# A gated cross-attention block on one core: scores transposed, probabilities kept in whole fp32, values weighed one step later

## Chip, cores and metric

One core of a Trainium2 chip runs the whole kernel. The metric is the device time of one launch in microseconds (us), the median of the runs shown. The launch holds every stage: query projection, attention, output projection and a small feed-forward part.

## What is computed

`x` is (8, 56, 512), the context is (8, 1500, 512), all in fp32. The attention has 32 query heads in 8 groups of 4; a group shares one key head and one value head of width 128. The mask here is all zeros, but it is added as given.

```python
q = rope(layernorm(x) @ wq)            # 8 x 56 rows, 32 heads of 128
k = rope(context @ wk)                 # 8 x 1500 rows, 8 heads of 128
v = context @ wv                       # 8 x 1500 rows, 8 heads of 128
attn = softmax(q k^T / sqrt(128) + mask)
x = x + tanh(g_xattn) * (attn v) @ wo
x = x + tanh(g_ffn) * lora_moe(layernorm(x))   # 4 experts, rank 16, top 2
```

## The kernel before, in words

**Precision.** A product that needs more than one reduced-precision pass is made of three: every operand is split into a high half (a copy rounded to fp32r) and a low half (the difference), and `PASSES` (line 45) sums hi x hi, low x hi and hi x low. K, V and the scores are made so. The high half is written by ScalarE and the low half by VectorE or GpSimd, mostly straight from PSUM.

**Stages.** `query_part` projects the queries of all batches and stores them by head group in DRAM. `attention_part` then runs 64 steps, one for each of 8 batches `b` and 8 groups `g`. `output_part` projects the stored attention output with `wo`, group by group, and adds the feed-forward part.

**One attention step** (`step`, one copy of it in each engine's program) works on group g and prepares the next one:
- *K parts* (`k_part`, L805): keys of the next group, 3 chunks of 500 positions (written K00 to K23: chunk, then quarter of the contraction), 3 matmuls of 500 columns each, 36 in all. ScalarE copies the halves of a chunk crosswise (swap, L715), VectorE multiplies by cosine and sine and adds (cos L938, sin L942, rot L948), ScalarE writes the high half (K, L720), GpSimd the low half (`k_low`, L673).
- *V parts* (`v_part`, L821): values for a pair of groups, made over two steps, on average 72 matmuls of 256 columns a step. ScalarE writes the high half (L734), VectorE the low half (`v_low`, L962).
- *Scores* (`scores`, L845): 112 rows (2 heads x 56 queries) by 500 keys, 6 such pieces (S0 to S5) of 3 matmuls. VectorE adds the mask and takes the row maximum in the same operation (L1002), then the maximum of three chunk maxima (L1007). ScalarE takes exp over 1500 columns with the row sum as a by-product (L760).
- *Transposes* (`transposes`, L857): the probabilities lie with queries on the partitions, and the product with the values needs keys there. Six groups T0 to T5 of four fp32 transposes each bring them to PSUM. ScalarE writes the high half (L785), VectorE the low half (L1027).
- *Weighing the values* (`weigh`, L874): for each of 12 tiles of 125 keys one matmul of v_hi against both halves (448 columns) and one of v_lo against the high half (224 columns); PV0 to PV5 are two tiles each. ScalarE and VectorE add the two 224-column results (L770, L1033).
- *Normalising* (`normalise`, L987): the row sums are inverted with the queries on the partitions (L1012), written to DRAM and read back spread over 128 partitions (`inv_dram`, two DMAs a step on SP's queue), and multiply the result of the step before. It is stored to DRAM for the output stage.
- In the last step of a batch (kind "turn") the context of the next batch is transposed as well, C0 to C11 of four transposes each (`c_transposes` L832, split at L724 and L953).

**What sets the order.** Each engine works through its own list for the kind of step: `PE_STEP`, `ACT_STEP`, `DVE_STEP` (from line 66 on), with kinds "even", "odd", "turn", "pre", "last" and a "first" list ahead of all. The lists are written out; a word is one piece of work, and every engine takes its list strictly in order, waiting on semaphores. PSUM is shared as rings of two banks: `k_banks`, `sv_banks` (scores and values), `t_banks` (context and probability transposes), `o_banks`. A ring's bank is handed back by `k_free`, `sv_free`, `t_free`, `o_free`.

**SP's queue** in a step: store the attention result of the step before (`store_attn`, L613), write and reread the inverted sums (L642), load the queries of the step after next, load two context tiles of the next batch. In the last batch it also starts the loads of the output stage.

**The output stage** (`project_group`, L1082): per group 4 heads x 4 column blocks x 3 matmuls of 448 columns; groups 0 and 1 are done within the last attention step (words O0 and O1 there), groups 2 to 7 after it. `split_low` on VectorE and `wo_high`/`attn_high` on ScalarE split each group's operands (L1059, L1053, L1071, L1065).

## Time and profile before

| | |
|---|---|
| runs shown | 2008.92, 2008.79, 2007.59 us; median 2008.79 us |
| profiled execution, first to last instruction (span) | 2005.4 us; its own launch time isn't listed, the medians lie 3.4 us above the span |
| TensorE matmul / weight load busy | 1976.7 us (99%) / 1775.9 us (89%) |
| VectorE / ScalarE / GpSimd busy | 1235.0 us (62%) / 1034.3 us (52%) / 311.6 us (16%) |
| mean granted TensorE clock | 0.996 |
| attention steps: first score matmul to first score matmul of the last step | 124.0 to 1882.2 us, 63 steps |
| HBM traffic | 76.6 MB read, 15.8 MB written |

How to read it: the records of matmuls overlap, because TensorE is pipelined. The duration of one record therefore says little, and the distance from one start to the next says what a matmul costs in a stream. In the tables of operands the moving operand stands first, then the stationary one; `112*125 112x112` is a stationary operand of 112 partitions by 125 columns and a moving one of 112 columns. A matmul of two plain fp32 operands (not fp32r) appears as two records, and a transpose of fp32 data as one: lines 1290 and 1275 issue 4 and 16 matmuls and have 8 and 32 records, line 857 issues 1536 transposes and has 1536. "PEclk" or "granted clock" is 1.00 at 2.4 GHz and 0.50 at 1.2 GHz.

### The profile page before, as it was taken

What the parts mean: (1) busy time and instruction counts of PE and PEld (TensorE: products, weight loads), DVE (VectorE), ACT (ScalarE), POOL (GpSimd) and SP (SyncE); (2) the same over time, 40 slices, a digit from 0 to 9 for tenths busy, and PEclk for the clock granted to TensorE, in tenths of its full rate; (3) what the DMA queues carried; (4) which work ended last, traced back from release to release, by engine and by line L of the source; (5) the groups of instructions that cost most, each with busy time, mean ns of one, the idle gap of its engine ahead of it and who ended that gap; (6) DMA issues with size and microseconds to landing.
All of it is one profiled execution on the core that took longest, in us unless ns stands there. A gap on an engine that the chain in (4) does not pass through costs nothing. (4 is left out here: it accounts for less than half of the span.)

```text
span 2005.4 us, 32965 instructions
## 1 busy us (share of the span) xinstructions
PE 1976.7 (99%) x12404; PEld 1775.9 (89%) x12404; DVE 1235.0 (62%) x2639; ACT 1034.3 (52%) x1754; POOL 311.6 (16%) x227
## 2 busy tenths in 40 slices
PE   7999999999999999999999999999999999999998
PEld 7989889988899988998899988998899998999786
DVE  6766556666666666666666666666665666566544
ACT  6655555554545555555644555455554555455532
POOL 5511111111111111111111111111111111111200
PEclk9999999999999999999999999999999999999998
DMA  7611212111211212221111112221111112121270
GB/s 227 248 56 35 35 18 44 35 31 20 43 10 33 36 17 44 35 35 20 39 19 25 35 20 41 36 35 20 39 25 26 28 20 41 36 33 15 48 263 19
DMA packets 74904, 94.41 MB, mean 47 GB/s; under 512 B 22692, under 2 KB 49444, under 8 KB 74760
## 3 DMA queue, kind: packets, MB, share of 16 engines
q1 hardware_dynamic: 73752, 86.01, 20.4%
q10 hardware_dynamic: 1008, 6.42, 0.8%
q8 instruction: 97, 1.59, 0.4%
q14 instruction: 47, 0.39, 0.1%
HBM read 76.64 MB, written 15.77 MB: 46 GB/s over the span
## 5 line engine op out<-in xcount | busy, mean ns | idle before, releaser
L673 POOL TENSOR_TENSOR k_lo<-k_work,k_hi 128x500 fp32r<-128x500 f32 x192 | 244.1, 1285 | 1541.0 <-ACT k_hi L720 1513.3
L821 PE MATMUL low_banks<-wv_hi,cT_hi 128*125 128x256 f32 x1536 | 443.1, 288 | 0.0
L821 PE MATMUL low_banks<-wv_hi,cT_lo 128*125 128x256 f32 x1536 | 431.0, 281 | 0.0
L821 PE MATMUL low_banks<-wv_lo,cT_hi 128*125 128x256 f32 x1536 | 430.9, 281 | 0.0
L1027 DVE TENSOR_TENSOR pT<-t_banks,pT 125x448 fp32r<-125x448 f32 x384 | 236.0, 622 | 242.8 <-ACT pT L785 242.8
L1002 DVE CUSTOM_DVE_ANT_0 prob<-low_banks,mask_t 112x500 f32<-112x500 f32 x384 | 259.1, 678 | 178.2 <-PE low_banks L845 176.9
L785 ACT ACTIVATE pT<-t_banks 125x448 fp32r<-125x448 f32 x384 | 205.1, 543 | 309.2 <-PE t_banks L857 308.2
L760 ACT ACTIVATE prob<-prob,neg_max 112x1500 f32<-112x1500 f32 x128 | 198.6, 1552 | 289.7 <-DVE neg_max L1007 288.9
L805 PE MATMUL low_banks<-cT_hi,wk_hi 128*128 128x500 f32 x768 | 312.0, 406 | 0.0
L805 PE MATMUL low_banks<-cT_hi,wk_lo 128*128 128x500 f32 x768 | 298.6, 389 | 0.0
L805 PE MATMUL low_banks<-cT_lo,wk_hi 128*128 128x500 f32 x768 | 298.3, 388 | 0.0
L821 PEld LDWEIGHTS low_banks<-wv_hi,cT_hi 128*125 128x125 f32 x1536 | 285.1, 186 | 4.3
L821 PEld LDWEIGHTS low_banks<-wv_hi,cT_lo 128*125 128x125 f32 x1536 | 285.8, 186 | 2.7
L821 PEld LDWEIGHTS low_banks<-wv_lo,cT_hi 128*125 128x125 f32 x1536 | 285.2, 186 | 0.0
L874 PE MATMUL o_banks<-pT,v_hi 125*128 125x448 f32 x768 | 272.4, 387 | 1.8 <-DVE pT L1027 0.7
L715 ACT ACTIVATE k_work<-low_banks 64x500 f32<-64x500 f32 x384 | 223.6, 582 | 14.4 <-PE low_banks L805 5.8
L857 PE MATMUL t_banks<-ident,prob 112*125 112x112 f32 x1536 | 220.6, 270 | 0.9 <-DVE pT L1027 0.9
L857 PEld LDWEIGHTS t_banks<-ident,prob 112*125 112x125 f32 x1536 | 207.0, 188 | 14.3 <-DVE pT L1027 1.0
L962 DVE TENSOR_TENSOR v_lo<-low_banks,v_hi 125x512 fp32r<-125x512 f32 x192 | 132.2, 689 | 137.0 <-ACT v_hi L734 137.0
L734 ACT ACTIVATE v_hi<-low_banks 125x512 fp32r<-125x512 f32 x192 | 114.3, 595 | 192.5 <-PE low_banks L821 192.3
L874 PE MATMUL o_banks<-pT,v_lo 125*128 125x224 f32 x768 | 193.5, 265 | 0.0
L805 PEld LDWEIGHTS low_banks<-cT_lo,wk_hi 128*128 128x128 f32 x768 | 144.5, 188 | 29.9
(136 smaller groups left out, 2910.2 us busy)
## 6 DMA issues: line engine op xcount, KB each, us to landing
stage<-in_ctx_dram SPq DMA_DIRECT2D x72, 250.0 KB
attn_by_head<-attn SPq DMA_DIRECT2D x65, 112.0 KB, 1.7
wq_raw<-in_L_xattn_wq_dram SPq DMA_DIRECT2D x7, 1024.0 KB, 7.2
q_raw<-q_by_head SPq DMA_DIRECT2D x64, 112.0 KB, 4.9
inv_b<-inv_by_head SPq DMA_DIRECT2D x64, 112.0 KB, 5.1
head_rows<-in_ctx_dram SPq DMA_DIRECT2D x24, 250.0 KB
mask_t<-in_mask_BxSxS_ff_dram SPq DMA_DIRECT2D x16, 328.1 KB
stage<-in_L_xattn_wo_dram SPq DMA_DIRECT2D x4, 1024.0 KB, 7.3
```

The costliest lines, as they stand in the source:

```text
L673: nc.gpsimd.tensor_tensor(k[1][:, c * SC:(c + 1) * SC], k_rot[:, s], f32(k[0][:, c * SC:(c + 1) * SC]), ALU.subtract).then_inc(k_lo, 1)
L715: nc.scalar.activation(k_swap[lo * HALF:(lo + 1) * HALF, s], k_banks[(1 - lo) * HALF:(2 - lo) * HALF, s, 0:SC], ACT.Copy).then_inc(k_swapp ...
L734: nc.scalar.activation(v[0][:, 2 * m:2 * m + 2, :], sv_banks[0:ST, m % 2, :].rearrange("p (t n) -> p t n", t=2), ACT.Copy).then_inc(v_hi, 1)
L760: nc.scalar.activation(prob[n][:, :], prob[n][:, :], ACT.Exp, bias=neg_max[:, n:n + 1], accum_out=row_sum[:, n:n + 1]).then_inc(p_ready, 1)
L785: nc.scalar.activation(pT[:, n % PT_SLOTS, :, 0, :], t_banks[0:ST, t_bank, 0:2 * GQ].rearrange("p (t n) -> p t n", t=2), ACT.Copy).then_in ...
L805: mm = nc.tensor.matmul(k_banks[:, s, 0:SC], w[0][a][:, d, g * DH:(g + 1) * DH], cT[m][:, d, c * SC:(c + 1) * SC], start=(d == 0 and n == ...
L821: mm = nc.tensor.matmul(sv_banks[0:ST, m % 2, t * PAIR:(t + 1) * PAIR], cT[a][:, d, tile * ST:(tile + 1) * ST], w[1][mv][:, d, g * DH:g * ...
L857: mm = nc.tensor.transpose(t_banks[0:ST, s, col:col + ROWS], prob[h][:, (2 * j + t) * ST:(2 * j + t + 1) * ST], ident[0:ROWS, 0:ROWS])
L874: mm = nc.tensor.matmul(o_banks[:, g % 2, 0:(2 - a) * GQ], v[a][:, 2 * j + t, (g % 2) * DH:(g % 2 + 1) * DH], probs, start=(first and a == ...
L962: nc.vector.tensor_tensor(v[1][:, 2 * m:2 * m + 2, :], sv_banks[0:ST, m % 2, :].rearrange("p (t n) -> p t n", t=2), f32(v[0][:, 2 * m:2 * ...
L1002: nc.vector.tensor_tensor_reduce(prob[h][:, c * SC:(c + 1) * SC], sv_banks[0:ROWS, n % 2, 0:SC], mask_t[:, c * SC:(c + 1) * SC], 1.0, LOWE ...
L1027: nc.vector.tensor_tensor(pT[:, n % PT_SLOTS, :, 1, :], t_banks[0:ST, t_bank, 0:2 * GQ].rearrange("p (t n) -> p t n", t=2), f32(pT[:, n % ...
```

## The change

The scores are made with the keys on the partitions: the stationary operand is a tile of 125 keys, the moving one the 224 query columns (4 heads x 56). Each of the six score pieces is now two key tiles, 6 matmuls of 224 columns, and the ring is `t_banks` instead of `sv_banks`. VectorE adds a mask that has been transposed once per batch (two items "B" of three transposes each in "first" and "turn", copied by VectorE), and writes the sums into one fp32 array `weights` (125 partitions x 25 slots x 224 columns, used by two steps in turn). The transposes of the probabilities and both splits of them are gone.

The maximum over the keys is found in four operations: over the first 8 tiles (max0), over the other 4 with the partial result (max1), transposed by TensorE to have queries on the partitions (MT, two transposes), reduced there ("rows", 2 x 125), and spread back over the partitions by two transposes of a broadcast column (MB). VectorE subtracts it from the scores in three operations of 896 columns (sub0 to sub2), ScalarE takes exp in three operations of 896 columns (exp0 to exp2). VectorE adds the 12 tiles in one `tensor_reduce` (total), and a matmul with ones (SUM) adds over the partitions and spreads the sums in one go; VectorE inverts them (inv) on 224 columns and multiplies (norm). The trip of the inverted sums through DRAM is gone.

Values and probabilities enter the last product in whole fp32: 12 matmuls of 224 columns into one bank, no low half of V, no second output half to add. This product, its sums, "inv" and "norm" of step n stand in the lists of step n+1 (words with a leading z). V parts V30 and V31 move from "first" to "zero", the kinds "zero" (g = 0), "pre" and "pre_last" (g = 6) get lists of their own. In the last step the product of that step follows within the same list, the heads of the output stage's first two groups are spread out (O00 to O13), and SP's loads for output group 3 stand behind the last store of the attention result. GpSimd's program changes only in the order of the last two steps. The mask is loaded as rows of 125 numbers.

```diff
 PE_STEP = {
...
-    "odd": ("S0 S1 K00 K01 S2 S3 K02 K03 S4 S5 K10 K11 K12 K13 K20 K21 T0 K22 T1 K23 T2 PV0 V00 T3 V01 PV1 PV2 V10 "
-            "T4 V11 PV3 V20 V21 T5 V30 V31 PV4 PV5"),
...
+    "zero": ("zPV0 K00 S0 S1 S2 zPV1 zPV2 zPV3 S3 S4 K01 S5 K02 K03 zPV4 zPV5 V30 K10 MT K11 K12 MB K13 zSUM V31 "
+             "V40 K20 K21 V41 K22 K23 V50 V51"),
+    "odd": ("K00 S0 S1 zPV0 zPV1 S2 S3 zPV2 S4 zPV3 zPV4 zPV5 K01 S5 zSUM K02 K03 K10 MT K11 K12 K13 MB V00 V01 "
+             "K20 K21 K22 K23 V10 V11 V20 V21"),
+    "even": ("zPV0 S0 zPV1 S1 S2 zPV2 S3 S4 K00 zPV3 zPV4 zPV5 zSUM S5 K01 K02 K03 K10 MT K11 K12 MB K13 V30 V31 "
+             "V40 K20 K21 K22 K23 V41 V50 V51"),
...
+    "turn": ("S0 S1 zPV0 S2 S3 zPV1 C0 S4 C1 zPV2 zPV3 S5 zPV4 C2 C3 zPV5 zSUM B0 K00 B1 C4 K01 K02 K03 MT C5 C6 "
+             "V00 MB C7 C8 V01 C9 K10 K11 K12 C10 V10 C11 V11 K13 K20 K21 K22 K23 V20 V21"),
...
+    "last": ("S0 S1 zPV0 S2 zPV1 S3 zPV2 S4 zPV3 S5 zPV4 zPV5 zSUM O00 MT O01 MB O02 O03 PV0 PV1 PV2 PV3 PV4 PV5 "
+             "O10 O11 SUM O12 O13"),
...
 ACT_STEP = {
...
-    "odd": "exp0 swap0 exp1 swap1 T0 T1 Q T2 T3 V0 T4 swap2 K0 V1 K1 T5 V2 V3 K2 out",
...
+    "odd": "Q swap0 swap1 K0 V0 exp0 exp1 exp2 V1 swap2 K1 K2 V2",
...
+    "turn": "C0 C1 C2 C3 C4 swap0 C5 C6 C7 C8 V0 C9 Q C10 C11 exp0 swap1 K0 swap2 exp1 exp2 V1 K1 K2 V2",
...
 DVE_STEP = {
...
-    "odd": ("mask0 mask1 mask2 max0 mask3 mask4 mask5 max1 norm cos0 sin0 inv T0 rot0 T1 T2 cos1 V0 sin1 rot1 T3 T4 Q V1 "
-            "cos2 T5 sin2 V2 rot2 V3 out"),
...
+    "zero": ("mask0 mask1 mask2 mask3 max0 mask4 mask5 max1 rows Q cos0 sin0 rot0 zinv sub0 sub1 sub2 sin1 cos1 "
+             "rot1 total cos2 znorm sin2 rot2"),
+    "odd": ("mask0 mask1 mask2 mask3 mask4 max0 mask5 max1 Q rows cos0 sin0 rot0 zinv sin1 sub0 sub1 znorm sub2 "
+             "cos1 rot1 total cos2 sin2 rot2"),
+    "even": ("mask0 mask1 mask2 mask3 mask4 max0 mask5 max1 rows zinv sub0 sin0 cos0 znorm rot0 cos1 Q sub1 sin1 "
+             "sub2 rot1 sin2 cos2 rot2 total"),
...
+    "turn": ("mask0 mask1 mask2 mask3 C0 mask4 max0 C1 mask5 C2 C3 B0 max1 B1 C4 zinv znorm rows C5 C6 cos0 C7 C8 "
+             "sin0 rot0 C9 Q sub0 sub1 C10 C11 sub2 cos1 sin1 rot1 cos2 sin2 rot2 total"),
...
+    "last": "mask0 mask1 mask2 mask3 max0 mask4 mask5 max1 zinv znorm rows sub0 sub1 sub2 total O1 inv norm",
...
...
-    v = halves("v", [ST, NT, PAIR])
+    v = [sb(f"v{u}", [ST, NT, PAIR]) for u in range(2)]
-    prob = [sb(f"prob{h}", [ROWS, SK]) for h in range(HALVES)]
-    pT = sb("pT", [ST, PT_SLOTS, 2, 2, GQ], F32R)
+    weights = sb("weights", [ST, 2 * NT + 1, GQ])
...
+                tile = slice((2 * j + t) * ST, (2 * j + t + 1) * ST)
+                for n, (a, m) in enumerate(PASSES):
+                    mm = nc.tensor.matmul(t_banks[0:ST, item % 2, t * GQ:(t + 1) * GQ], k[a][:, tile], q[m][:, :],
+                                          start=(n == 0), stop=(n == len(PASSES) - 1))
+        def turn_max(n):
+            pe.wait_ge(max_ready, n + 1)
+            if n:
+                pe.wait_ge(p_shifted, n * GROUPS)
+            for h in range(HALVES):
+                mm = nc.tensor.transpose(m_bank[0:ROWS, h * ST:(h + 1) * ST], key_max[:, h * ROWS:(h + 1) * ROWS], ident[0:ST, 0:ST])
+            mm.then_inc(max_turned, 1)
+        def spread_max(n):
+            pe.wait_ge(rows_ready, n + 1)
+            for h in range(HALVES):
+                mm = nc.tensor.transpose(m_bank[0:ST, h * ROWS:(h + 1) * ROWS], row_max[:, h:h + 1].broadcast_to([ROWS, ST]),
+                                         ident[0:ROWS, 0:ROWS])
+            mm.then_inc(max_spread, 1)
+        def spread_sums(n):
+            pe.wait_ge(sum_ready, n + 1)
+            pe.wait_ge(ones_ready, 1)
+            pe.wait_ge(attn_ready, n + 1)
+            nc.tensor.matmul(sums_b, ones[:, :], tile_sum[:, :], start=True, stop=True, skip_group_check=True).then_inc(sums_spread, 1)
+        def weigh(n, j):
+                pe.wait_ge(attn_ready, n + 1)
+            pe.wait_ge(p_exp, n * GROUPS + (j // GROUP + 1))
+            if n % 2 == 0:
+                pe.wait_ge(v_free, v_item(n // 2, j) + (RING + 1))
+            probs = pair_weights(n, j)
+                mm = nc.tensor.matmul(o_acc, v[n // 2 % 2][:, 2 * j + t, (n % 2) * DH:(n % 2 + 1) * DH], probs[:, t],
+                                      start=(j == 0 and t == 0), stop=(j == PT - 1 and t == 1), skip_group_check=True)
+            mm.then_inc(p_weighed, 1)
...
+        def add_mask(b, g, j, last):
+            n, item = b * HKV + g, t_item(b, g, "S", j, last)
+            four = "p t (h s) -> p t h s"
+            if j == 0:
+                last_part = t_item(b - 1, HKV - 1, "B", MASK_ITEMS - 1) if b else T_FIRST - 1
+                dve.wait_ge(t_free, last_part + (RING + 1))
+            dve.wait_ge(t_ready, item + 1)
+            if n >= 2 and j == 0:
+                dve.wait_ge(p_weighed, (n - 1) * PT)
+                dve.wait_ge(sum_ready, n - 1)
+            nc.vector.tensor_tensor(pair_weights(n, j).rearrange(four, h=REP),
+                                    t_banks[0:ST, item % 2, 0:2 * GQ].rearrange("p (t h s) -> p t h s", t=2, h=REP),
+                                    mask_keys[:, j, :, None, :].broadcast_to([ST, 2, REP, SQ]), ALU.add).then_inc(t_free, 1)
+        def max_begin(b, g, last):
+            dve.wait_ge(t_free, t_item(b, g, "S", SHIFTED - 1, last) + (RING + 1))
+            if b * HKV + g:
+                dve.wait_ge(max_ready, b * HKV + g)
+            nc.vector.tensor_reduce(weights[:, NT, :], pair_weights(b * HKV + g, 0, SHIFTED).rearrange("p t q -> p q t"),
+                                    AX_X, ALU.max).then_inc(max_begun, 1)
+        def max_end(b, g, last):
+            n = b * HKV + g
+            dve.wait_ge(t_free, t_item(b, g, "S", PT - 1, last) + (RING + 1))
+            dve.wait_ge(max_begun, n + 1)
+            first = 2 * SHIFTED if n % 2 == 0 else NT
+            nc.vector.tensor_reduce(key_max[:, :], weights[:, first:first + 2 * GROUP + 1, :].rearrange("p t q -> p q t"),
+                                    AX_X, ALU.max).then_inc(max_ready, 1)
+        def max_rows(n):
+            dve.wait_ge(max_turned, n + 1)
+            nc.vector.tensor_reduce(row_max[:, :], m_bank[0:ROWS, 0:HALVES * ST].rearrange("p (h k) -> p h k", h=HALVES),
+                                    AX_X, ALU.max).then_inc(rows_ready, 1)
+        def shift(n, j):
+            dve.wait_ge(max_spread, n + 1)
+            group = pair_weights(n, j * GROUP, GROUP)
+            nc.vector.tensor_tensor(group, group, max_b[:, None, :].broadcast_to([ST, 2 * GROUP, GQ]), ALU.subtract).then_inc(p_shifted, 1)
+        def sum_keys(n):
+            dve.wait_ge(p_exp, (n + 1) * GROUPS)
+            if n:
+                dve.wait_ge(sums_spread, n)
+            first = (n % 2) * (NT + 1)
+            nc.vector.tensor_reduce(tile_sum[:, :], weights[:, first:first + NT, :].rearrange("p t q -> p q t"),
+                                    AX_X, ALU.add).then_inc(sum_ready, 1)
+        def invert_sums(n):
+            dve.wait_ge(sums_spread, n + 1)
+            dve.wait_ge(p_weighed, (n + 1) * PT)
+            dve.wait_ge(attn_ready, n + 1)
+            nc.vector.reciprocal(inv_b[:, :], sums_b).then_inc(inv_ready, 1)
+        def normalise(n):
+            dve.wait_ge(inv_ready, n + 1)
+            dve.wait_ge(attn_stored[(n + 1) % 2], 16 * (n // 2 + 2))
+            nc.vector.tensor_tensor(o_sum[:, :], o_acc, inv_b[:, :], ALU.mult).then_inc(attn_ready, 1)
...
+                    act.wait_ge(p_shifted, n * GROUPS + (j + 1))
+                    group = pair_weights(n, j * GROUP, GROUP)
+                    nc.scalar.activation(group, group, ACT.Exp).then_inc(p_exp, 1)
...
-                store_attn(b, g)
-
-                wait_apart(sp, inv_ready, b * (HKV * HALVES) + (g + 1) * HALVES, sp_passed)
-                with nc.allow_non_contiguous_dma("224 numbers"):
-                    sp.dma_start(inv_dram[g].rearrange("h r -> r h"), inv_sum[:, :]).then_inc(inv_stored, 16)
-                wait_apart(sp, inv_stored, b * (16 * HKV) + 16 * (g + 1), sp_passed)
-                sp.dma_start(inv_b[:, :], inv_dram[g:g + 1].rearrange("g h r -> g (h r)").broadcast_to([P, GQ])).then_inc(inv_loaded, 16)
...
+                store_attn(b, g)
...
-        output_loads(sp, shared, wo, attn_dram, 0, sp_passed)
+        output_load(sp, shared, wo, attn_dram, 0, 0, sp_passed)
         store_attn(B, 0)
+        output_load(sp, shared, wo, attn_dram, 0, 1, sp_passed)
```

## Rows read from the trace of the kernel before

**Rows 1.** A stretch: length; busy PE, PEld, DVE, ACT, POOL; clock; DMA share; GB/s
```profile
102.00:1882.00 1780.00, 1775.32 (x11393) 1599.83 (x11392) 1108.04 (x2433) 931.84 (x1617) 245.17 (x193) 1.00 0.18 30
```

**Rows 2.** Instructions of L845: durations in ns, first and last start in us
```profile
L845 PE MATMUL low_banks<-k_hi,q_hi x384: 382/388/641, 124.0 to 1889.9; 128*112 128x500 f32 x192
```

**Rows 3.** Timeline of the last step, with what TensorE waited for
```profile
1882.24 0.39 PE L845 MATMUL low_banks<-k_hi,q_hi 128*112 128x500 f32 x1
...
1885.28 0.45 PE L845 MATMUL low_banks<-k_hi,q_hi 128*112 128x500 f32 x1 [2.19 <-POOL k_lo L673]
...
1891.99 0.45 PE L1082 MATMUL low_banks<-cT_hi,wk_hi 128*128 128x448 f32 x1 [0.98 <-DVE chunk_max L1002]
```

**Rows 4.** Timeline of TensorE within one step: start, duration, instruction
```profile
603.49 0.40 PE L805 MATMUL low_banks<-cT_hi,wk_hi 128*128 128x500 f32 x1
...
607.34 0.38 PE L805 MATMUL low_banks<-cT_lo,wk_hi 128*128 128x500 f32 x1
607.56 0.59 PE L857 MATMUL t_banks<-ident,prob 112*125 112x112 f32 x4
607.91 0.47 PE L805 MATMUL low_banks<-cT_hi,wk_hi 128*128 128x500 f32 x1
608.22 0.39 PE L805 MATMUL low_banks<-cT_hi,wk_lo 128*128 128x500 f32 x1
...
614.13 0.37 PE L874 MATMUL o_banks<-pT,v_hi 125*128 125x448 f32 x1
...
615.38 0.29 PE L821 MATMUL low_banks<-wv_hi,cT_hi 128*125 128x256 f32 x1
...
619.30 0.29 PE L821 MATMUL low_banks<-wv_hi,cT_hi 128*125 128x256 f32 x1
...
622.15 0.59 PE L857 MATMUL t_banks<-ident,prob 112*125 112x112 f32 x4
```

**Rows 5.** Timeline of the last 20 us: the matmuls of two plain fp32 operands
```profile
1988.19 1.80 PE L1275 MATMUL low_banks<-arT,yT 128*112 128x68 f32 x16
...
1994.81 7.17 PE L1290 MATMUL low_banks<-bT,midT 64*112 64x512 f32 x8 [0.71 <-DVE midT L1355]
```

**Rows 6.** Three stretches, the first two those of Rows 5; granted clock third from the end
```profile
1988.00:1990.00 2.00, 1.99 (x20) 1.82 (x18) 0.00 (x0) 1.59 (x2) 0.00 (x0) 1.00 0.03 8
1995.00:2002.00 7.00, 6.97 (x8) 2.10 (x8) 2.25 (x3) 0.00 (x0) 0.00 (x0) 0.50 0.23 69
1887.00:1890.00 3.00, 3.00 (x9) 1.86 (x8) 1.59 (x7) 1.36 (x1) 3.00 (x4) 0.52 0.68 233
```

**Rows 7.** Groups of VectorE by form: busy us, mean ns, idle before
```profile
L1027 DVE TENSOR_TENSOR pT<-t_banks,pT 125x448 fp32r<-125x448 f32 x384 | 236.0, 622 | 242.8 <-ACT pT L785 242.8
L962 DVE TENSOR_TENSOR v_lo<-low_banks,v_hi 125x512 fp32r<-125x512 f32 x192 | 132.2, 689 | 137.0 <-ACT v_hi L734 137.0
L942 DVE TENSOR_TENSOR k_work<-k_work,k_tables 128x500 f32<-128x500 f32 x192 | 128.5, 669 | 0.0
L987 DVE TENSOR_TENSOR attn<-o_sum,inv_b 128x224 f32<-128x224 f32 x65 | 25.3, 389 | 0.0
L1012 DVE RECIPROCAL inv_sum<-row_sum 112x1 f32<-112x1 f32 x128 | 16.3, 153 | 4.0 <-ACT prob L760 1.3
L1071 DVE TENSOR_TENSOR wk_lo<-k_work,wk_hi 128x2048 fp32r<-128x2048 f32 x4 | 9.2, 2293 | 16.6 <-ACT wk_hi L1059 16.6
L1346 DVE RECIPROCAL inv_total<-total 112x4 f32<-112x4 f32 x1 | 0.2, 177 | 0.0
```

**Rows 8.** Groups of ScalarE and GpSimd by form
```profile
L760 ACT ACTIVATE prob<-prob,neg_max 112x1500 f32<-112x1500 f32 x128 | 198.6, 1552 | 289.7 <-DVE neg_max L1007 288.9
...
L724 ACT ACTIVATE cT_hi<-t_banks 128x500 fp32r<-128x500 f32 x96 | 52.0, 589 | 32.0 <-PE t_banks L832 31.3
...
L673 POOL TENSOR_TENSOR k_lo<-k_work,k_hi 128x500 fp32r<-128x500 f32 x192 | 244.1, 1285 | 1541.0 <-ACT k_hi L720 1513.3 <-DMA q_by_head<-q_rot 27.7
```

**Rows 9.** DMA issues of the page: size, median us from issue to landing
```profile
stage<-in_L_xattn_wo_dram SPq DMA_DIRECT2D x4, 1024.0 KB, 7.3
```

More of the change, by code:

```diff
@@ L139, in k_item, with t_item, v_item, next_pair @@
     return b * K_ITEMS + g * NC + c
[L142 to L159 removed]
+def t_item(b, g, what, n, last=False):
+    return b * T_ITEMS + (T_FIRST + g * PT + t_place(step_kind(g, last), what, n))
+def v_item(pair, m):
+    return pair * VT + m
+def next_pair(step):
+    return (step + step % 2) // 2
 def wait_apart(eng, sem, value, passed):
@@ L880, in _ @@
         query_tensor(pe, c_transposes)
         pe.wait_ge(shared.w_lo, HKV)
-        for what, n in tasks(PE_STEP["first"]):
+        for what, ago, n in tasks(PE_STEP["first"]):
             if what == "V" and n[0] < RING and n[1] == 0:
@@ new lines, in step @@
+            for what, ago, (j, *_) in tasks(DVE_STEP[step_kind(g, last)]):
+                n = b * HKV + g - ago
+                if n < 0:
+                    continue
+                s = ((g + 1) * NC + j) % 2
+                if what == "mask":
+                    add_mask(b, g, j, last)
+                if what == "max":
+                    (max_end if j else max_begin)(b, g, last)
+                if what == "rows":
+                    max_rows(n)
+                if what == "sub":
+                    shift(n, j)
+                if what == "total":
+                    sum_keys(n)
@@ L1178, in _ @@
         with sp.Fori(1, pairs - 1) as i:
[L1179 removed]
+            for u in range(2):
+                output_load(sp, shared, wo, attn_dram, i, u, sp_passed)
         for t in range(NTT):
```

444 lines of the change are left out of this document (208 added, 236 removed), and 36 rows, old and new, of tables (ACT_STEP, DVE_STEP, PE_STEP).

## Prediction

> **What bounds the kernel now.** I read the busy time of the long middle stretch first: TensorE is busy 1775.3 of 1780.0 us at a granted clock of 1.00, VectorE 1108.0, ScalarE 931.8 [rows 1]. Then TensorE's timeline: from one start to the next nothing is left over, whichever kind follows which [rows 4]. The first score matmul stands at 124.0 us and that of the last step at 1882.2 [rows 2, 3], so 63 steps take 27.9 us each. The other engines count only where their order makes TensorE wait.
>
> As overlapping records say little, I price a matmul by distances between starts [rows 4]. K: 17 matmuls in 603.49 to 607.34, 0.2265 us each for 500 columns, or 0.453 ns a column; score matmuls have the same width and the same price. Values: 24 in 619.30 to 622.15, 0.119. A weighing pair (448 and 224 columns): four in 614.13 to 615.38, 0.313. A group of four transposes: the K matmul behind it starts early and is drawn out, so I take 607.56 to 608.22 less one K, 0.43, or 0.108 a transpose. Check: 36 K (8.15), 72 value matmuls (8.55), 18 scores (4.08), six transpose groups (2.60), 12 pairs (3.75) and an eighth of twelve context groups (0.65) make 27.8 against the measured 27.9. The step is the sum of its matmuls.
>
> **TensorE's part, per step.** K and V parts keep their number (V30 and V31 only move to step "zero"). Removed: scores 4.08, transposes 2.60, pairs 3.75, together 10.43 us.
>
> Added:
> - Scores, 36 matmuls of 224 columns. By the column rate 0.101 us each; the V row, 256 columns, gives 0.119 as upper end. The nearest sign of a floor for a new stationary operand: 16 records of only 68 columns take 1.80 us less a tail, some 0.107 each, at full clock [rows 5, 6]. I take 0.106: 3.82 (3.64 to 4.28).
> - Weighing, 12 whole fp32 matmuls of 224 columns, two records each. The only wide case is L1290: 8 records of 512 columns in 7.17 us at granted clock 0.50 [rows 5, 6], at most 0.896 each, or 2.1 cycles a column at 1.2 GHz. At 2.4 GHz two cycles a column give 0.187, the row with its tail 0.196, and two columns at the K rate 0.203. I take 0.190: 24 x 0.190 = 4.56 (4.48 to 4.90).
> - SUM, one fp32 matmul of 224 columns: 0.38.
> - MT and MB, four transposes at 0.108: 0.43. Six mask transposes per batch: 0.08 a step.
>
> Together 9.27 (8.97 to 10.1). TensorE gains 1.16 us a step (0.33 to 1.46), over 64 steps 74 us (21 to 93).
>
> **VectorE's part.** Its own rows give a fixed 0.15 us and 1.05 ns a column (389 ns for 224, 2293 for 2048) [rows 7]. Now it works 1108.0/63.8 = 17.4 us a step [rows 1], of it six probability splits at 0.62 and three v_lo at 0.69 that go. Afterwards: six mask additions of 448 at 0.62 = 3.7 (the broadcast mask is read at the same column count; I add nothing, at worst twice the time); max0 over 1792 numbers 2.0, max1 over 1120 1.3, "rows" 0.4, total over 2688 3.0; three subtractions of 896 at 1.09 = 3.3; norm and Q 0.8; nine K operations at 0.67 = 6.0; twelve context splits and two mask copies a batch, 1.1 a step. The reciprocal of 224 numbers costs 0.4 like norm; the rows show it only for 1 and 4 numbers, 153 and 177 ns [rows 7], 8 ns a further number, which would be 1.9. I take 0.4 and keep 1.9 as the end. Sum 22.0 (with the slow reciprocal 23.5) of a new step of 27.9 - 1.16 = 26.7: 82% instead of 62%, no bound, but hardly any cover left for delays. On that operation the Trainium skill (VectorE: DVE Perf Modes, The fixed hardware budget) says that reciprocal is an iterative divide with a repeat count of 8; whether that means eight cycles a number no run here shows, and if it does the end of 1.9 us holds.
>
> **ScalarE and GpSimd.** ScalarE loses the six probability splits and "out", and three exps of 896 at about 1.0 us replace two of 1.55 [rows 8]: it becomes lighter. GpSimd's three k_lo of 1.29 us [rows 8] stay. Both cost nothing, since TensorE's K for the next step ends 5 us or more ahead of the score that needs it (K23, then V41 V50 V51 at 1.4 each, then the next step's S0 to S3 and PV).
>
> **SP's queue.** Two DMAs and three waits a step go. `store_attn` now stands behind the query and context loads and waits for znorm, in the middle of the step; the loads queued behind it are for two steps later. The mask of the next batch, in pieces of 500 bytes, is loaded in step 0 and first read in step 7, 180 us later. Cost nothing. In the last step the loads of output group 3 stand behind the last store. From that norm to their split halves I count 0.4 for the store's issue, some 8 us of loading (7.3 from issue to landing for wo alone [rows 9]) and 4 of splits, against O12, O13 and group 2, 72 matmuls of 448 columns at 0.203 by the K rate, 14.6 us: just covered. If that cover fails, a few microseconds, once.
>
> **Where the order makes TensorE wait.** I laid the engines' lists for "odd", "even" and "turn" side by side with the prices above. In "odd", S5 ends at 9.7 us; mask5, max1 and the hand-overs take 2.1, while SUM K02 K03 K10 stand between, 2.4: MT finds its operand by 0.3. MB has 2.0 us of K against 0.9 for Q and "rows". "total" ends with the step, so the next mask0 starts 0.0 to 0.5 late and S2, behind two PVs, doesn't notice. "even" looks the same. The step "turn" is the exception: 12 context splits raise VectorE to 30 of 31.8 us. C1 needs the bank of C0, whose two splits (0.59 and 0.67, behind mask3) [rows 7, 8] last 1.3 us, and only S4 (0.64) stands between: 0.7 us. Its total ends about 36 us after the start, 3 after TensorE is done with the step, and S2 of the next step waits 1.3 for mask0. Two us in each of 7 turns, 14, and 1 elsewhere: +15 us (0 to 45).
>
> **The two ends.** "first" gains six mask transposes, counted. In the last step TensorE now waits 2.19 us for k_lo, 0.98 before O0, and works 3 us at clock 0.52 [rows 3, 6]. PVs between the scores and k_lo ahead of GpSimd's wo work take away some 5 us of that; O10 comes too early for O1, which stands behind total: 2 us back. Together -3 (-6 to +3).
>
> **Sum.** -74 + 15 - 3 = -62 us; the span goes from 2005.4 to 1943. The median of the runs lies 3.4 above the span, so the forecast is 2008.8 - 62 = 1947 us.
>
> **Rivals.**
> 1. *New waits at the maximum.* MT's cover of 0.3 us in half of the steps is smaller than what I can't see: if mask additions take 0.15 us more each, or a wait stands behind the 2-us operations, MT or S4 waits 0.3 to 0.9 us in each step. For it: five engine changes in a row, S5, mask5, max1, MT, rows, MB. Against: TensorE keeps six K or V parts to fill with, and hand-overs in the timeline cost below 0.1. At 0.5 us a step: +32, 1979 us.
> 2. *The reductions run at half rate, and VectorE becomes the bound.* max0, max1 and total read along keys with 896 bytes from one number to the next; no row here reads SBUF so, all long ones read neighbours [rows 7]. Its place is VectorE in every step; its price is 5600 numbers at another 1.05 ns, 5.9 us. That makes 27.9 us of VectorE work, over the 26.7 of TensorE, and as VectorE idles at least 1 us a step waiting for MT, MB and exp2, the step is 28.9 to 29.5: 64 x 1.0 more than now or worse, 2075 us. It decides from about 4.7 us more per step. Against: every fp32 row runs at one number a cycle or less, whatever its operands. The Trainium skill has a rule for exactly this (Advanced Engine Details and Errata, SBUF Cachelines): accesses that each fall in another 16-byte line pay a penalty. By that rule the change would come out slower.
> 3. *The fp32 product at its upper prices*, with scores at 0.119: gain 21 instead of 74 us, 2000 us; it would take both ends at once.
>
> **Chances.** Forecast with its own bounds (1922 to 1968) 0.62; rival 1 (1968 to 1995) 0.20; rival 2 0.12; rival 3 near the old time 0.03; still faster than 1922 0.03. The range leaves out rivals 2 and 3 and the fast end, 0.18: 1922 to 1995. A measurement of this kernel tells 0.2%, 4 us, from no change; only rival 3 and the mild end of rival 2 fall there, 0.04 together, so faster has 0.85 and slower 0.11.
>
> **What the profile after would show.** Distances of 0.10 to 0.107 between score matmuls; records of the weighing 0.19 apart; TensorE still busy 98% or more; VectorE about 80% in the middle; total near 3.0 us and max0 near 2.0; idle time of TensorE at C1 of the turns and at the following S2. A total near 5.8 us proves rival 2; TensorE waits on key_max or row_max, rival 1; weighing records above 0.2, the upper price. What would make it wrong at once: VectorE above 95%.

## Result and the profile after

The changed kernel takes 2082.03 us (median of 4 runs, 2079.64 to 2085.70) against 2008.72 for the kernel before in the same comparison: ratio 1.0368, 95% interval 1.0353 to 1.0383. It is slower by 73 us. The forecast of 1947 and its range to 1995 are missed; rival 2 had said 2075.

The page after, its first part (busy time, share of the span, instructions):

```profile
span 2079.0 us, 31832 instructions
## 1 busy us (share of the span) xinstructions
PE 1949.9 (94%) x12452; PEld 1786.4 (86%) x12452; DVE 1783.7 (86%) x1886; ACT 782.4 (38%) x1242; POOL 318.4 (15%) x227
```

The middle, first in a stretch that answers to [rows 1] (it ends 7 us behind the last score matmul), then from the first score matmul to that of the last step, 63 steps; columns as in [rows 1]:

```profile
102.00:1960.00 1858.00, 1753.85 (x11482) 1613.04 (x11481) 1656.91 (x1700) 684.89 (x1114) 260.80 (x200) 0.99 0.08 25
122.20:1945.10 1822.90, 1726.65 (x11312) 1589.44 (x11311) 1633.27 (x1670) 671.07 (x1092) 246.42 (x188) 0.99 0.07 23
```

TensorE was busy all but 5 of 1780 us; now it idles 104 of 1858. VectorE went from 62% to 89%. The span grew by 73.6 us. A step takes 1822.9/63 = 28.9 us instead of 27.9, of which VectorE works 1633.3/63 = 25.9; the 63 steps make 65 of the 73.6 us.

VectorE's groups by form, after; they answer to [rows 7]:

```profile
L1078 DVE TENSOR_REDUCE tile_sum<-weights 125x224 f32<-125x2688 f32 x64 | 325.3, 5082 | 1.0 <-ACT weights L780 1.0
L1039 DVE TENSOR_TENSOR weights<-t_banks,mask_keys 125x448 f32<-125x448 f32 x384 | 232.0, 620 | 109.5 <-PE t_banks L871 106.3
L1048 DVE TENSOR_REDUCE weights<-weights 125x224 f32<-125x1792 f32 x64 | 213.5, 3336 | 0.3
L1069 DVE TENSOR_TENSOR weights<-weights,m_bank 125x896 f32<-125x896 f32 x192 | 201.0, 1072 | 8.2 <-PE m_bank L889 8.2
L1057 DVE TENSOR_REDUCE key_max<-weights 125x224 f32<-125x1120 f32 x64 | 136.9, 2139 | 1.7
L1086 DVE RECIPROCAL inv_b<-o_bank 128x224 f32<-128x224 f32 x64 | 99.1, 1549 | 7.2 <-PE o_bank L898 7.2
L1062 DVE TENSOR_REDUCE row_max<-m_bank 112x2 f32<-112x250 f32 x64 | 26.6, 416 | 21.8 <-PE m_bank L882 21.8
L1092 DVE TENSOR_TENSOR o_sum<-o_bank,inv_b 128x224 f32<-128x224 f32 x64 | 24.5, 383 | 0.3
```

The total takes 5.08 us for 2688 numbers, 1.89 ns each, max0 3.34 (1.86) and max1 2.14 (1.91). The forecast had 1.05 to 1.17 ns and 6.3 us for the three; they take 10.56. The reciprocal takes 1.55 us instead of 0.4. Mask addition, subtraction, "rows" and norm stand where they were put.

TensorE's longest sums of waits after: what it waited for, us in total, times, longest:

```profile
PE t_banks L871 <- DVE weights L1039: 48.4, 48, 3.1
PE m_bank L882 <- DVE key_max L1057: 31.6, 56, 1.6
PE t_banks L848 <- DVE cT_lo L999: 12.0, 16, 0.8
PE o_bank L909 <- DVE o_sum L1092: 4.7, 7, 0.7
```

The first is S2 waiting for the first mask addition, which stands behind the total of the step before; the second is the transpose of the maximum, MT, waiting for max1. One place in the timeline, where a step "turn" hands over to the next (start, duration, instruction, wait before it):

```profile
1046.58 4.91 DVE L1078 TENSOR_REDUCE tile_sum<-weights 125x224 f32<-125x2688 f32 x1
...
1051.40 1.15 DVE L1039 TENSOR_TENSOR weights<-t_banks,mask_keys 125x448 f32<-125x448 f32 x2
1052.08 0.28 PEld L871 LDWEIGHTS t_banks<-q_hi,k_hi 128*125 128x125 f32 x1 [3.32 <-DVE weights L1039]
1052.08 0.55 PE L871 MATMUL t_banks<-q_hi,k_hi 128*125 128x224 f32 x1 [3.14 <-DVE weights L1039]
```

Stretches around that wait, columns as in [rows 1]:

```profile
1046.00:1048.00 2.00, 2.00 (x14) 1.88 (x13) 2.00 (x2) 2.00 (x5) 0.51 (x1) 1.00 0.00 0
1048.00:1051.00 3.00, 0.94 (x9) 0.76 (x7) 3.00 (x1) 0.41 (x1) 1.97 (x2) 1.00 0.20 45
1051.60:1053.00 1.40, 0.92 (x4) 0.92 (x5) 0.96 (x2) 0.00 (x0) 0.00 (x0) 0.50 0.75 200
1053.00:1057.00 4.00, 4.00 (x14) 3.68 (x13) 0.62 (x1) 0.00 (x0) 0.00 (x0) 0.50 0.30 106
```

TensorE idles three microseconds, and the 6 us of work behind them, up to 1058.1 us, run at a granted clock of 0.50, which is 1.2 GHz: the wait is paid a second time. The low clock comes seven times, once behind each turn, and makes 34 us in all, of which up to half are lost. Over the whole span the mean granted clock is 0.987.

### The profile page after: what moved, and what is told of

The parts are those of the page before. It is cut to its first block and busy times, and to the rows that moved or that the text cites. A ratio compares the mean times of both kernels' runs of the same rounds, so it can differ in the third digit from the quotient of the medians.

```text
span 2079.0 us, 31832 instructions
## 1 busy us (share of the span) xinstructions
PE 1949.9 (94%) x12452; PEld 1786.4 (86%) x12452; DVE 1783.7 (86%) x1886; ACT 782.4 (38%) x1242; POOL 318.4 (15%) x227
## 5 line engine op out<-in xcount | busy, mean ns | idle before, releaser
L685 POOL TENSOR_TENSOR k_lo<-k_work,k_hi 128x500 fp32r<-128x500 f32 x192 | 251.5, 1313 | 1609.9 <-ACT k_hi L737 1580.3
L909 PE MATMUL o_bank<-weights,v 125*128 125x224 f32 x1536 | 341.5, 364 | 4.7 <-DVE o_sum L1092 4.7
L1078 DVE TENSOR_REDUCE tile_sum<-weights 125x224 f32<-125x2688 f32 x64 | 325.3, 5082 | 1.0 <-ACT weights L780 1.0
L1039 DVE TENSOR_TENSOR weights<-t_banks,mask_keys 125x448 f32<-125x448 f32 x384 | 232.0, 620 | 109.5 <-PE t_banks L871 106.3
L909 PEld LDWEIGHTS o_bank<-weights,v 125*128 125x128 f32 x1536 | 286.0, 196 | 11.7 <-DVE o_sum L1092 7.1
L871 PE MATMUL t_banks<-q_hi,k_hi 128*125 128x224 f32 x768 | 236.3, 308 | 49.6 <-DVE weights L1039 48.4
L1048 DVE TENSOR_REDUCE weights<-weights 125x224 f32<-125x1792 f32 x64 | 213.5, 3336 | 0.3
L871 PE MATMUL t_banks<-q_hi,k_lo 128*125 128x224 f32 x768 | 210.6, 274 | 0.0
L871 PE MATMUL t_banks<-q_lo,k_hi 128*125 128x224 f32 x768 | 210.5, 274 | 0.0
L1069 DVE TENSOR_TENSOR weights<-weights,m_bank 125x896 f32<-125x896 f32 x192 | 201.0, 1072 | 8.2 <-PE m_bank L889 8.2
L780 ACT ACTIVATE weights<-weights 125x896 f32<-125x896 f32 x192 | 175.9, 947 | 37.1 <-DVE weights L1069 35.9
```

What stands on the lines that cost most here:

```text
L685: nc.gpsimd.tensor_tensor(k[1][:, c * SC:(c + 1) * SC], k_rot[:, s], f32(k[0][:, c * SC:(c + 1) * SC]), ALU.subtract).then_inc(k_lo, 1)
L780: nc.scalar.activation(group, group, ACT.Exp).then_inc(p_exp, 1)
L871: mm = nc.tensor.matmul(t_banks[0:ST, item % 2, t * GQ:(t + 1) * GQ], k[a][:, tile], q[m][:, :], start=(n == 0), stop=(n == len(PASSES) - 1))
L909: mm = nc.tensor.matmul(o_acc, v[n // 2 % 2][:, 2 * j + t, (n % 2) * DH:(n % 2 + 1) * DH], probs[:, t], start=(j == 0 and t == 0), stop=(j ...
L1039: nc.vector.tensor_tensor(pair_weights(n, j).rearrange(four, h=REP), t_banks[0:ST, item % 2, 0:2 * GQ].rearrange("p (t h s) -> p t h s", t ...
L1048: nc.vector.tensor_reduce(weights[:, NT, :], pair_weights(b * HKV + g, 0, SHIFTED).rearrange("p t q -> p q t"), AX_X, ALU.max).then_inc(ma ...
```

## Experiments

The theory after the result: the three reductions, which read with 896 bytes from one number to the next, cost almost twice the forecast, and that alone turned the sign. The rivals: another new operation (the reciprocal), or a single wait at one place, not VectorE's work as a whole. Each experiment is an edit of the changed kernel, and each is compared with the kernel before.

**1. The reductions read neighbours.** One view more, used by one or more of the three reductions. It reads as many numbers from the same tiles, but next to each other, so that one output mixes queries:

```diff
+    def near(tiles, count):
+        return tiles.rearrange("p t q -> p (t q)").rearrange("p (q t) -> p q t", t=count)
...
-            nc.vector.tensor_reduce(tile_sum[:, :], weights[:, first:first + NT, :].rearrange("p t q -> p q t"),
+            nc.vector.tensor_reduce(tile_sum[:, :], near(weights[:, first:first + NT, :], NT),
                                     AX_X, ALU.add).then_inc(sum_ready, 1)
```

The sums are then those of other queries. For the maximum a query is shifted by another constant, which its division takes out again.

The total alone:

> Leaves the sums wrong: total adds the same 2688 numbers, but twelve neighbours at a time instead of one number out of each tile. Theory A (VectorE's work sets the step, the far-apart reads cost it): total falls from 5.08 to about 3.0 us, 2.1 us less VectorE work a step. TensorE's own sum is 26.9 us a step against 28.9 measured, so at most 2.0 us a step can come back; as waits at the turn stay, 1.3 to 1.9 us: 1960 to 2000 us. Theory B (what counts is the chain from the last mask addition over max1, MT, rows and MB, which TensorE stands and waits for): total is not in that chain, 2060 us or more. Theory C (the pattern of the read costs nothing, the reduction itself is slow at this size): total stays at 5.1 us and the time at 2082.

Both maxima:

> Leaves the maxima wrong: max0 and max1 read the same count of numbers, but neighbours. Theory A: max0 falls from 3.34 to 2.0 and max1 from 2.14 to 1.3, together 2.1 us a step, the same amount as for total alone, so the time is that of the run with total alone within 10 us, 1960 to 2000 us. Theory B: the gain is here and not there, 1960 to 1990 us while total alone stays above 2060. Theory C: no change of the durations, 2082 us.

All three:

> Leaves maxima and sums wrong: all three long reductions read neighbours. Theory A: VectorE loses 4.2 us a step, falls well under TensorE, and the step ends at TensorE's sum of 26.9 us plus the waits of the turns: 1950 to 1975 us. Theory B: the same as with the maxima alone. Theory C: 2082 us.

Measured: total near 2001.60 us (ratio 0.9965, 0.9951 to 0.9979), maxima near 2024.59 (1.0076, 1.0059 to 1.0093), all near 1951.66 (0.9721, 0.9704 to 0.9737). That is 80, 57 and 130 us less than the changed kernel. All near lies in theory A's range. The total misses its range by 2 us, and the maxima miss theirs (1960 to 2000, within 10 us of the total) by 25. The reductions with all near, by form:

```profile
L1081 DVE TENSOR_REDUCE tile_sum<-weights 125x224 f32<-125x2688 f32 x64 | 188.4, 2944 | 1.0 <-ACT weights L783 1.0
L1051 DVE TENSOR_REDUCE weights<-weights 125x224 f32<-125x1792 f32 x64 | 128.7, 2011 | 0.3
L1060 DVE TENSOR_REDUCE key_max<-weights 125x224 f32<-125x1120 f32 x64 | 83.9, 1312 | 1.7
```

And what TensorE still waits for in its middle, then the 63 steps (columns as in [rows 1]), 26.9 us each:

```profile
PE t_banks L874 <- DVE weights L1042: 8.2, 7, 1.2
PE t_banks L851 <- DVE cT_lo L1002: 5.2, 7, 0.7
```

```profile
122.82:1819.60 1696.78, 1681.65 (x11312) 1581.37 (x11311) 1376.58 (x1673) 670.74 (x1092) 256.50 (x188) 1.00 0.08 25
```

Nothing but the addresses of three reads was changed, the reductions fell to the forecast's durations, and the time fell to 5 us from the forecast. The two waits that are left are those the forecast had named, the S2 behind each turn (1.2 us, forecast 1.3) and C1 within it (0.7, forecast 0.7), seven times each. The single edits are nearly additive (80 + 57 = 137 against 130), so neither wait hid the other. With the total near the wait for mask additions falls from 48 to 8 us and that for key_max stays at 31; with the maxima near it is the other way round, 48 us of the first and none of the second. Where I had expected the two single edits to be worth the same, they differ by 23 us for equal VectorE time (2.14 and 2.16 us a step); experiment 2 asks why.

**2. max1 alone reads neighbours**, max0 and the total as in the changed kernel; the same edit at one place.

> Of the changed kernel, the second reduction for the maximum (max1, 1120 numbers, behind the last mask addition) alone reads neighbours; max0 and the total stay 896 bytes apart. max1 should fall from 2139 to 1312 ns, 0.83 us per step, max0 stay at 3336 and the total at 5082. Both maxima near gave -57 us for 2.16 us per step; with the total 28 bytes apart and max0 alone at full rate the time fell by only about 9 us for 1.0 us per step. Theory A, time follows VectorE's work wherever it stands: 0.83 of 2.16, so 22 us less than the changed kernel, 2060 us. Theory B, time follows the place: the turn of the maximum waits for max1 alone, which stands right behind the last scores, while max0 stands in a gap in which VectorE waits for scores anyway; then max1 carries most of the 57 us: 40 to 55 us less, 2027 to 2042 us, and TensorE's wait for key_max is all but gone (31.6 us in the changed kernel).

Measured: 2038.15 us (1.0148, 1.0131 to 1.0165), 44 less than the changed kernel; max1 1312 ns, max0 3335. TensorE's waits:

```profile
PE t_banks L874 <- DVE weights L1042: 46.7, 45, 3.1
PE t_banks L851 <- DVE cT_lo L1002: 10.5, 14, 0.8
PE o_bank L912 <- DVE o_sum L1095: 4.7, 7, 0.7
PE m_bank L885 <- DVE key_max L1060: 2.3, 9, 0.8
```

Theory B holds. 0.83 us a step at max1 is worth 44/64 = 0.69; the other 1.33 us, at max0, are worth (57 - 44)/64 = 0.2. A shorter max0 makes VectorE wait longer for the next scores: from 130 to 1900 us 97 us with max1 alone, 146 with both maxima near. The total's 2.14 are worth 1.25. So "VectorE is the bound" was only half of it: it is busy 89%, TensorE 94%, and each waits for the other in turn. What a microsecond costs is set by the place it stands in.

**3. The reciprocal**, once in the changed kernel and once with all reductions near. The edit leaves the division out: the sum itself is copied, so the output is scaled wrongly.

```diff
-            nc.vector.reciprocal(inv_b[:, :], sums_b).then_inc(inv_ready, 1)
+            nc.vector.tensor_copy(inv_b[:, :], sums_b).then_inc(inv_ready, 1)
```

> Leaves the inversion out: a copy of 224 numbers stands for the reciprocal (1.55 us by the trace). Theory A: 1.2 us less VectorE work a step, of which nearly all comes back: 2010 us (2000 to 2030). Theory B: in the odd and even lists zinv stands behind max1, so little comes back, 2060 us or more.

> Leaves maxima, sums and inversion wrong: near_all with a copy for the reciprocal. Theory A as mended (the slow reciprocal lies in the gap in which VectorE would wait for MB, and with VectorE under its bound nothing of it shows): 1950 us, within 4 of near_all. Rival (the 1.2 us that the copy saves was held up by the long reductions and appears now): 1900 to 1930 us, which TensorE's sum forbids.

Measured: 2062.91 us (1.0270, 1.0253 to 1.0287) in the changed kernel, 19 less; 1950.46 (0.9711, 0.9695 to 0.9727) with the reductions near, 1 less. The copy takes 382 ns, so 1.17 us a step go, 75 in all. For the first, theory A's 2010 us are a miss, and theory B's "2060 us or more" came; the second came as theory A has it. VectorE's waits that grew with the copy, from 130 to 1900 us:

```profile
DVE cT_lo L999 <- ACT cT_hi L741: 26.9, 35, 1.2
DVE k_work L985 <- ACT k_work L732: 26.8, 40, 0.8
DVE weights L1069 <- PE m_bank L889: 18.7, 23, 0.9
```

In the changed kernel they were 20.3, 12.5 and 5.2 us in the same stretch, 34 less. The third is the first subtraction waiting for MB; it takes up 13.5 of the 56 us that do not come back, and waits for ScalarE take up 21. Another part was never in the step's sum: VectorE's busy time falls by 53 us over the 63 steps (1633 to 1581), not by 74, as its neighbouring records overlap. As the reason for the lost sign the reciprocal falls.

**4. From which distance on does a read cost more?** Two kernels with the three reductions 8, 16, 28 and 32 bytes apart, one run of each. As in experiment 1, an output mixes queries.

```diff
+    def apart(tiles, count, step):
+        return tiles.rearrange("p t q -> p (t q)").rearrange("p (a t b) -> p a b t", t=count, b=step)
...
-            nc.vector.tensor_reduce(tile_sum[:, :], weights[:, first:first + NT, :].rearrange("p t q -> p q t"),
+            nc.vector.tensor_reduce(split(tile_sum[:, :], 2), apart(weights[:, first:first + NT, :], NT, 2),
                                     AX_X, ALU.add).then_inc(sum_ready, 1)
```

> Leaves maxima and sums wrong, to read the price of distance: total takes numbers 8 bytes apart, max0 16 bytes apart, max1 32 bytes apart. Theory A1 (any step beyond the neighbour costs): all three at 1.86 ns a number, 5.08, 3.34 and 2.14 us. Theory A2 (the price starts where each number falls in a line of its own of 16 bytes): total near 2.95 us, max0 3.3 and max1 2.1. Theory A3 (only a far distance costs, as 896 bytes): all three as with neighbours, 2.95, 2.0 and 1.3 us.

> Leaves maxima and sums wrong. The distances change places: total 28 bytes, max0 8 bytes, max1 16 bytes. If the distance alone decides and the step lies between 8 and 16 bytes: total 5.1 us, max0 2.0, max1 2.1. If the operation or its length decides: total stays near 2.95 and max0 near 3.3 as in the first ladder. Time: total costs 2.1 us more and max0 1.3 less a step than in the first ladder, 2020 to 2045 us.

Measured (mean ns of one, and that over the numbers read):

| bytes apart | reduction | ns | ns a number |
|---|---|---|---|
| 4 | total, max0, max1 | 2944, 2011, 1312 | 1.10, 1.12, 1.17 |
| 8 | total, max0 | 2943, 2011 | 1.09, 1.12 |
| 16 | max0, max1 | 3361, 2196 | 1.88, 1.96 |
| 28 | total | 5344 | 1.99 |
| 32 | max1 | 2235 | 2.00 |
| 896 | total, max0, max1 | 5082, 3336, 2139 | 1.89, 1.86, 1.91 |

8 bytes cost nothing and 16 nearly the whole; no run has 12. The price is 0.7 to 0.9 ns a number. The Trainium skill (Advanced Engine Details and Errata, SBUF Cachelines) says that at least two hits on a line of 16 bytes are needed to hide the access; the table agrees.

The times were 2010.08 us (8, 16 and 32 bytes) and 2073.33 us (28, 8 and 16). The second was expected at 2020 to 2045 and missed: max0 was the reduction made fast there, and by experiment 2 that one is worth 0.2 us a step, while the total became slower by 0.26.

**5. The reductions as additions of whole tiles.** The maximum and the sum by VectorE's elementwise operation on pairs of tiles, which read neighbours; nothing is left out.

```diff
-            nc.vector.tensor_reduce(tile_sum[:, :], weights[:, first:first + NT, :].rearrange("p t q -> p q t"),
-                                    AX_X, ALU.add).then_inc(sum_ready, 1)
+            pairs = [weights[:, first + 2 * j:first + 2 * j + 2, :] for j in range(PT)]
+            for j in range(1, PT):
...
+                nc.vector.tensor_tensor(adding[:, :, :], adding[:, :, :] if j > 1 else pairs[0], pairs[j], ALU.add).then_inc(sum_steps, 1)
...
+            nc.vector.tensor_tensor(tile_sum[:, :], adding[:, 0, :], adding[:, 1, :], ALU.add).then_inc(sum_ready, 1)
```

> Right results: maximum and sum by additions and maxima of two tiles against two tiles, 448 neighbours each, five and one of 224 for each, in place of the three reductions. VectorE: 3.5 instead of 5.5 us for the maximum, 3.5 instead of 5.1 for the sum, 3.6 us less a step. Theory A: nearly the gain of the reductions that read neighbours, 1955 to 1985 us. Rival (a chain of dependent operations costs a hand-over each, about 0.1 us, and the maximum's last part stands on the path): 1990 to 2010 us.

Measured: 2047.24 us (1.0198, 1.0181 to 1.0215), a miss of both ranges. VectorE's groups by form, of the same shape, the upper one additions, the lower one maxima:

```profile
L1093 DVE TENSOR_TENSOR adding<-adding,weights 125x448 f32<-125x448 f32 x256 | 225.9, 882 | 8.8
...
L1056 DVE TENSOR_TENSOR halving<-halving,weights 125x448 f32<-125x448 f32 x128 | 81.9, 640 | 4.4
```

A maximum costs 640 ns a pair, an addition 882. It is not the operation: the first addition of a step takes 615. The additions run at the end of the step, while GpSimd makes k_lo, and they are of two kinds: the others take 626 ns in the median and up to 1585. So the sum takes 0.62 + 4 x 0.88 + 0.50 = 4.6 us instead of 5.08, hardly a gain, and TensorE waits 57.4 us for mask additions (longest 3.8). The hand-overs of the rival are small, 8.8 us in all ahead of the 256 additions.

**6. The sum on GpSimd**, the maximum by pairs on VectorE; once with the additions between the k_lo, and once with k_lo ahead of them.

```diff
-    "odd": "klo0 klo1 klo2",
+    "odd": "klo0 klo1 add1 add2 add3 klo2 add4 add5 add6",
```

> Right results: the maximum by pairs on VectorE, the sum by pairs on GpSimd, which is busy 15%; five additions of 448 numbers at 1.15 us and one of 224 at 0.6 by its own rows, 6.4 us a step beside three k_lo of 1.3. VectorE loses 7 us a step. Theory A: TensorE's sum is the bound, 1945 to 1960 us, under both kernels. Rival (GpSimd and VectorE slow each other where both read and write SBUF, and k_lo comes late): VectorE's rows for SBUF operands grow by over 10%, 1970 us or more.

```diff
-    "odd": "klo0 klo1 add1 add2 add3 klo2 add4 add5 add6",
+    "odd": "klo0 klo1 add1 klo2 add2 add3 add4 add5 add6",
```

> Right results: the kernel with the sum on GpSimd again, with every k_lo ahead of the additions but one. There TensorE waited 43.6 us for k_lo. If late k_lo was what kept it at 2014 us: 1955 to 1975 us, and the idle time before scores released by k_lo near 0. If the two engines' contention does it: 2000 us or more, with k_lo waits gone and others in their place.

Measured: 2014.46 us (1.0030, 1.0019 to 1.0040) and 2020.45 (1.0062, 1.0047 to 1.0078). Theory A and the late k_lo are missed; the rival with the contention came in both. TensorE's first wait, in the one and in the other:

```profile
PE t_banks L893 <- POOL k_lo L689: 43.6, 46, 1.4
```

```profile
PE o_bank L920 <- POOL adding L719: 31.1, 23, 1.7
```

GpSimd takes 1151 ns for an addition (VectorE 615), and VectorE's operations beside them grow: the first of the step's pairwise maxima takes 1055 instead of 629 ns on average. One place in the first kernel's timeline:

```profile
537.07 1.14 POOL L716 TENSOR_TENSOR adding<-adding,weights 125x448 f32<-125x448 f32 x1
537.49 1.19 DVE L1071 TENSOR_TENSOR halving<-weights 125x448 f32<-125x448 f32 x1
538.28 0.93 POOL L719 TENSOR_TENSOR adding<-adding 125x224 f32<-125x224 f32 x1
```

GpSimd's addition ends at 538.21 and VectorE's maximum half a microsecond later, at 538.68; alone it takes 0.63 in all. It is the same everywhere: in the three kernels with pairs, each of the 325 pairwise operations of 448 numbers on VectorE that take over 0.7 us ends 0.48 to 0.49 us behind the end of a GpSimd operation. So VectorE's operation does not run more slowly beside GpSimd's, it waits for the end of it. k_lo first removes the wait for k_lo and makes TensorE wait for the sum. Neither of the two orders brings both early enough.

**7. The tiles stored in pairs.** If two hits in 16 bytes are enough, the tiles of two neighbouring key blocks can be interleaved number by number: a reduction reads two neighbours, then jumps 1792 bytes. Nothing is left out. The other places only change their views, and one unused place is filled once with a very low number. TensorE now reads the probabilities 8 bytes apart.

```diff
-    weights = sb("weights", [ST, 2 * NT + 1, GQ])
+    weights = sb("weights", [ST, 2 * PT + 1, GQ, 2])
...
-                mm = nc.tensor.matmul(o_acc, v[n // 2 % 2][:, 2 * j + t, (n % 2) * DH:(n % 2 + 1) * DH], probs[:, t],
+                mm = nc.tensor.matmul(o_acc, v[n // 2 % 2][:, 2 * j + t, (n % 2) * DH:(n % 2 + 1) * DH], probs[:, 0, :, t],
...
-            nc.vector.tensor_reduce(tile_sum[:, :], weights[:, first:first + NT, :].rearrange("p t q -> p q t"),
-                                    AX_X, ALU.add).then_inc(sum_ready, 1)
+            nc.vector.tensor_reduce(tile_sum[:, :], weights[:, first:first + PT].rearrange("p j q t -> p q j t"),
+                                    AX_XY, ALU.add).then_inc(sum_ready, 1)
```

> Right results, and the three reductions kept: the two tiles of a pair lie interleaved in SBUF, number by number, so that a reduction reads two neighbours (8 bytes) and then jumps. The reader of the last product and the mask addition step by 8 bytes in turn. Theory A2 (two numbers of one 16-byte line per visit are enough, as the ladder shows 8 bytes apart at full rate): total 2.95, max0 2.0, max1 1.6 us (it reads 1344 numbers now), weighing records still 0.19 us apart, and the time that of near_all, 1948 to 1960 us, under both kernels. Rival (a jump costs wherever it falls, half as often here): total near 4 us, 1990 to 2030 us. Second rival (TensorE pays for its 8-byte step): weighing records at 0.22 us or more apart, 46 us or more on top.

Measured: 1967.23 us (0.9799, 0.9786 to 0.9813), 2% faster than the kernel before, with right results. The reductions came as expected, the time misses its range (1948 to 1960) by 7 us. VectorE's groups by form, then TensorE's waits in the middle:

```profile
L1080 DVE TENSOR_REDUCE tile_sum<-weights 125x224 f32<-125x2688 f32 x64 | 188.4, 2944 | 1.0 <-ACT weights L781 1.0
...
L1050 DVE TENSOR_REDUCE weights<-weights 125x224 f32<-125x1792 f32 x64 | 128.7, 2012 | 0.3
...
L1059 DVE TENSOR_REDUCE key_max<-weights 125x224 f32<-125x1344 f32 x64 | 98.8, 1545 | 1.7
```

```profile
PE t_banks L872 <- DVE weights L1041: 7.9, 7, 1.1
PE t_banks L849 <- DVE cT_lo L1002: 5.2, 7, 0.7
```

The full rate at 1792 bytes from pair to pair, and no waits but those of experiment 1. The 16 us over all near are TensorE's, the second rival at a third of its price: its weighing records follow each other after 199 ns instead of 189. In the timelines eight of them take 1.75 us here and 1.68 with all near:

```profile
1002.61 1.75 PE L910 MATMUL o_bank<-weights,v 125*128 125x224 f32 x8
```

```profile
996.08 1.68 PE L912 MATMUL o_bank<-weights,v 125*128 125x224 f32 x8
```

1536 records by 10 ns are 15 us. So the layout has a price too, on the engine that is now the bound, but a small one.

## Why the prediction was wrong

**The step that failed** is one sentence of VectorE's part: the reductions priced at the rate of rows that read neighbours ("max0 over 1792 numbers 2.0, max1 over 1120 1.3, 'rows' 0.4, total over 2688 3.0"). The access was new, [rows 7] could say nothing of it, and the forecast took the near end of its bounds with a reason ("every fp32 row runs at one number a cycle or less") that held only for rows that read neighbours. Measured: 10.56 us for the three instead of 6.3. Experiment 1 puts only this back and gets 1951.7 us against 1947.

**TensorE's part was right.** Distances after, medians: scores 110 ns (forecast 106, inside 101 to 119), weighing records 189 (190). With all near TensorE is busy 99.1% of the 63 steps. The scores' 4 ns by 36 by 64 are 9 us lost, the waits 13 instead of 15.

**The term for the two ends had the wrong sign, at a small price.** From the first score matmul of the last step to the end it takes 123.2 us before and 130.4 with all near, 7.2 more. The product of the step before, which now stands there too (4.56 + 0.38), less the step's own gain (1.16) are 3.8 of it, so the end costs 3.4 us, where the forecast had -3. The wait for k_lo is gone and O10 waits, both as foreseen; no term had O00 waiting for GpSimd's low half of the attention output. With all near, O00 and then O10:

```profile
1832.71 0.45 PE L1177 MATMUL low_banks<-cT_hi,wk_hi 128*128 128x448 f32 x1 [3.60 <-POOL cT_lo L700]
1851.11 0.47 PE L1177 MATMUL low_banks<-cT_hi,wk_hi 128*128 128x448 f32 x1 [1.82 <-DVE cT_lo L1160]
```

The 5 us between 1947 and 1952 can lie in this and in the scores.

**Rival 2 was right in kind and, by luck, in size** (2075 against 2082). It had the reductions 5.9 us dearer and VectorE at 27.9 us a step with 1 us of idling. They are 4.3 dearer, VectorE is busy 25.9 and idles 3.0. One part of that is in the forecast's own sum, which added mean durations although neighbouring records overlap by some 0.1 us: with all near VectorE is busy 1376.6/63 = 21.9 us a step, where the sum with the reciprocal at 1.55 gives 23.2. The rival's threshold, 4.7 us more per step, was wrong too: with the reciprocal copied, the 4.3 of the reductions alone still give 2063 us, since waits arise at S2 and MT long before VectorE is full.

**Rival 1's wait came, from rival 2's cause.** MT waits 31.6 us, 56 times, up to 1.6 us; with max1 at 1.31 it is 2.3 us. With max1 as priced, the cover of 0.3 us that the forecast counted there was enough.

**The reciprocal** stood at 0.4 with 1.9 as the end; it takes 1.55, or (1549 - 153)/223 = 6.3 ns a number beyond the first, against 1.05 for a plain operation: six times; the forecast's end had 8 ns a number. It cost 1 us in all where VectorE had room, and 19 where it had not (experiment 3).

**Where the 130 us between the changed kernel and all near lie:** the waits of the middle, 96.7 us in the four rows above against 13.4, make 83. The lower clock behind them makes about (0.995 - 0.987) x 2079 = 17, by the mean granted clocks of the two runs. The other 30 are not assigned. Matmul records overlap, so waits read from them come out too short (3.14 where the weight load shows 3.32): by the weight loads the waits for mask additions and key_max alone are 67 and 55 us in the changed kernel, against 48 and 32. How much of that is lost time is not separated.

**The chances.** I gave the cause that came true 0.12 although the rows could not speak against it and the rule of the Trainium skill that I named (Advanced Engine Details and Errata, SBUF Cachelines) spoke for it. A price with no row of its own, multiplied by 5600 numbers a step on an engine with 18% of room, should have weighed as much as the forecast.

## What to carry to other kernels

Before a reduction moves to another axis, look at the bytes between the numbers it reads in sequence: with fp32 on VectorE numbers 4 or 8 bytes apart ran at full rate, those 16 bytes or more apart at little over half. Interleaving tiles in pairs restored the rate for 5% on the matmul that reads them. And price an operation by what waits behind it: in this kernel 1 us taken from max1 was worth 0.8, from the total 0.6, from the reciprocal 0.25 and from max0 0.15.
